# Second pass of a two-stage vision block: who issues the copies of the attention heads' operands

## The reference

```python
qkv = (x.reshape(B, L, dim) @ w_qkv + b_qkv).reshape(B, L, 3, nh, hd)
q = rot(q); k = rot(k)
attn = jnp.einsum('bnqd,bnkd->bnqk', q, k) * scale
rel_h = jnp.einsum('bnhwc,hkc->bnhwk', q6, bias_h)
rel_w = jnp.einsum('bnhwc,wkc->bnhwk', q6, bias_w)
attn = attn.reshape(B, nh, H, W, H, W) + rel_h[..., :, None] + rel_w[..., None, :]
attn = jax.nn.softmax(attn.reshape(B, nh, L, L), axis=-1)
out = jnp.einsum('bnqk,bnkd->bnqd', attn, v)
...
x = x + _L0_conv_ref(_gn(x), ...)
x = x + _L1_conv_ref(_gn(x), ...)
```

## Time and profile before

| | us |
|---|---|
| median of 3 runs | 3322.99 (3320.98 to 3324.75) |
| profiled execution, its own time | 3324.98 |
| its span, first to last instruction | 3323.2 |
| PE busy | 2701.7 (81%) |
| DVE busy | 2407.5 (72%) |
| ACT busy | 1554.1 (47%) |
| POOL busy | 1345.9 (41%) |
| mean granted TensorE clock | 0.932 |

### The profile page before, as it was taken

One profiled execution on the slowest core, in us unless ns is written; L12 is line 12 of the kernel. 1 busy time (PEld: TensorE's weight loads), 2 busy tenths in 40 slices (PEclk: granted clock), 3 DMA queues, 4 the chain that ended last, 5 costly groups with the idle time before them and its releaser, 6 DMA issues. The chain is left out here.

```text
span 3323.2 us, 40828 instructions
## 1 busy us (share of the span) xinstructions
PE 2701.7 (81%) x15888; PEld 1340.8 (40%) x15888; DVE 2407.5 (72%) x2270; ACT 1554.1 (47%) x1908; POOL 1345.9 (41%) x636
## 2 busy tenths in 40 slices
PE   3577777888778876777667998989888999989889
PEld 1222223333223332222223555546554555556555
DVE  1698899998999999999983555646554555636555
ACT  4445643556435564444431445525553445525554
POOL 4478766887668876766652100011000200011000
PEclk8799998998999999999896999999999999999999
DMA  2334444454444544445542112020021111020110
GB/s 68 120 120 133 146 144 142 133 138 154 148 144 128 139 158 143 161 133 145 178 136 68 22 33 52 10 62 11 23 52 40 32 33 28 25 71 1 33 52 20
DMA packets 96358, 297.46 MB, mean 90 GB/s; under 512 B 18860, under 2 KB 21432, under 8 KB 96152
## 3 DMA queue, kind: packets, MB, share of 16 engines
q1 hardware_dynamic: 96152, 294.68, 29.3%
HBM read 238.51 MB, written 23.07 MB: 79 GB/s over the span
## 5 line engine op out<-in xcount | busy, mean ns | idle before, releaser
L1605 POOL TENSOR_TENSOR arena<-arena 128x1024 f32<-128x1024 f32 x384 | 902.6, 2362 | 332.1 <-DVE arena L1093 280.6
L1093 DVE TENSOR_TENSOR_SCAN arena<-PS,arena 128x1024 f32<-128x1024 f32 x384 | 878.1, 2287 | 89.7 <-ACT PS L1442 63.8
L567 PE MATMUL PS<-arena,ident 128*128 128x512 f32 x1568 | 812.9, 645 | 20.5 <-ACT arena L1453 15.6
L1442 ACT ACTIVATE PS<-arena,a_inf,a_neg 128x1024 f32<-128x1024 f32 x384 | 463.8, 1208 | 777.0 <-DVE arena L1093 772.6
L1221 DVE CUSTOM_DVE_ANT_1 arena<-PS,arena 128x1024 f32<-128x1024 f32 x384 | 468.2, 1219 | 417.0 <-PE PS L852 415.4
L1530 ACT ACTIVATE arena<-arena,neg_max 128x1024 f32<-128x1024 f32 x384 | 440.9, 1148 | 577.9 <-DVE neg_max L1221 577.9
L558 PE MATMUL PS<-arena,sel 96*128 96x512 bf16 x768 | 247.0, 405 | 407.2 <-DVE arena L1101 403.8
L852 PE MATMUL PS<-arena 64*128 64x512 f32 x1536 | 448.5, 661 | 80.4 <-DMA arena<-arena 76.3
L1635 POOL TENSOR_TENSOR arena<-arena 128x512 f32<-128x512 f32 x48 | 68.4, 1424 | 1067.5 <-ACT arena L1499 1067.5
L1101 DVE TENSOR_TENSOR arena<-arena,PS 128x1024 f32<-128x1024 f32 x384 | 459.2, 1196 | 15.6 <-PE PS L558 13.9
L567 PEld LDWEIGHTS PS<-arena,ident 128*128 128x128 f32 x1568 | 319.6, 205 | 307.1 <-issue 250.2
(11 more groups left out here) (124 smaller groups left out, 2177.6 us busy)
## 6 DMA issues: line engine op xcount, KB each, us to landing
arena<-b_rows SPq DMA_DIRECT2D x256, 512.0 KB, 3.8
arena<-b_rows SPq DMA_DIRECT2D x256, 256.0 KB, 4.0
arena<-arena SPq DMA_DIRECT2D x216, 64.0 KB, 2.3
arena<-arena SPq DMA_DIRECT2D x96, 128.0 KB, 3.0
normed<-xn SPq DMA_DIRECT2D x5, 1536.0 KB, 6.4
normed<-x_in SPq DMA_DIRECT2D x4, 1536.0 KB, 7.6
residual<-x_in SPq DMA_DIRECT2D x4, 1536.0 KB, 8.3
x<-residual SPq DMA_DIRECT2D x4, 1536.0 KB, 6.4
```

Of the source, the lines that this page charges most:

```text
L567: last = pe.matmul(dst[:, half(h)], lhs, rhs[:, half(h)], start=start, stop=stop, skip_group_check=True)
L1093: dve.tensor_tensor_scan(HS[:, at % 2, ::step], DA[:, ::step], DBU[:, at % R3, ::step], 0.0, ALU.mult, ALU.add).then_inc(scan_done.sem, 1)
L1442: act.activation(DA, DELTA[:, tile % 2, :], ACT.Exp, bias=a_inf[:, col:col + 1], scale=a_neg[:, col:col + 1]).then_inc(da_ready.sem, 1)
L1605: pool.tensor_tensor(DBU[:, at % R3, :], DU[:, tile % 2, :], BSB[:, at % R3, :], ALU.mult).then_inc(dbu_ready.sem, 1)
```

## The change

Heads 0 and 1 stay with SP. The ten DMAs of heads 2 and 3 are issued by POOL, with the same waits ahead of them, in its own program order: the q copies after its addition `n` = 1, the k and bias copies after `n` = 3, group 1 after `n` = 9 and group 2 after `n` = 11. `head_loaded[2]` and `head_loaded[3]` are moved ahead of the semaphores that are cleared for each image; they are kept over the images, so whoever waits for them compares with `(b * 30 + n) * 16`, a value that is computed from the loop's register.

```diff
-    def __init__(self, sem, unit=1):
-        self.sem, self.unit = sem, unit
+    def __init__(self, sem, unit=1, kept=None):
+        self.sem, self.unit, self.kept = sem, unit, kept
     def after(self, b, n):
-        return n * self.unit
+        return n * self.unit if self.kept is None else (b * self.kept + n) * self.unit
...
+        head_loaded = [None] * (HG // 2) + [
+            Signal(ctx.enter_context(nc.semaphore(f"head{j}_loaded")), 16, HEAD_DMAS * GROUPS) for j in range(HG // 2, HG)]
...
-        head_loaded = [signal(f"head{j}_loaded", HEAD_DMAS * GROUPS, 16) for j in range(HG)]
+        head_loaded[0:HG // 2] = [signal(f"head{j}_loaded", HEAD_DMAS * GROUPS, 16) for j in range(HG // 2)]
...
+        OWN_HEADS = {"sp": range(HG // 2), "pool": range(HG // 2, HG)}
...
                 for k, (ready, count) in enumerate(((rope_ready, 2), (rope_ready, 4), (rel_saved, 2))):
                     sp.wait_ge(ready.sem, ready.after(b, count))
-                    for j in range(HG):
+                    for j in OWN_HEADS["sp"]:
                         for dst, src in operands(0, j)[k]:
                             sp.dma_start(dst, src).then_inc(head_loaded[j].sem, 16)
                 for g in range(1, GROUPS):
                     sp.wait_ge(rope_ready.sem, rope_ready.after(b, ROPE_FOR[g]))
                     sp.wait_ge(rel_saved.sem, rel_saved.after(b, REL_FOR[g]))
-                    for j in range(HG):
+                    for j in OWN_HEADS["sp"]:
...
+                def load_first(k):
+                    ready, count = ((rope_ready, 2), (rope_ready, 4), (rel_saved, 2))[k]
+                    pool.wait_ge(ready.sem, ready.after(b, count))
+                    for j in OWN_HEADS["pool"]:
+                        for dst, src in operands(0, j)[k]:
+                            pool.dma_start(dst, src).then_inc(head_loaded[j].sem, 16)
+                def load_group(g):
+                    pool.wait_ge(rope_ready.sem, rope_ready.after(b, ROPE_FOR[g]))
+                    pool.wait_ge(rel_saved.sem, rel_saved.after(b, REL_FOR[g]))
+                    for j in OWN_HEADS["pool"]:
+                        pool.wait_ge(s_psum.sem, s_psum.after(b, STEPS * g - HG + j + 1))
+                        for dst, src in itertools.chain(*operands(g, j)):
+                            pool.dma_start(dst, src).then_inc(head_loaded[j].sem, 16)
...
+                    if n in (1, 3):
+                        load_first(n // 2)
+                    if n == 3:
+                        load_first(2)
+                    if n in (9, 11):
+                        load_group(1 if n == 9 else 2)
```

More of the change, by code:

```diff
@@ L375, in build, with operands @@
         LATE_AT = {2 * m + 2: job for m, job in enumerate(LATE) if job}
+        def operands(g, j):
+            copies = [[], [], [(QX[2 * HD * h + HD:2 * HD * h + 2 * HD, j, :], RELC[j::HG, g // 2, :])
+                               for h in range(2)]]
+            for h in range(2):
+                for odd in range(2):
+                    at = XT * odd + HALF_HEAD * j
+                    rows = slice(2 * HD * h + HALF_HEAD * odd, 2 * HD * h + HALF_HEAD * (odd + 1))
+                    copies[0].append((QX[rows, j, :], QKC[at:at + HALF_HEAD, PLACE[g, "q"], :]))
+                    copies[1].append((KX[rows, j, :], QKC[at:at + HALF_HEAD, PLACE[g, "k"], half(h)]))
+            return copies
+        OWN_HEADS = {"sp": range(HG // 2), "pool": range(HG // 2, HG)}
         def norm_count(g, h):
```

## The result

The changed kernel takes 3296.6 us (median of 4 runs, 3295.6 to 3303.1) against 3323.4 before: a ratio of 0.9924, 95% interval 0.9907 to 0.9941. It is 27 us faster where 12 us slower was forecast.

A forecast was written before the change was run, and what follows sets the result against it. Bound: SP's issuing of 40 DMAs at each of eight group changes. Changes +14, image starts -3, register waits +1 make +12 us on the 3323 us median: 3335 us, range 3262 to 3412 (eight in ten).

The forecast's parts named there:

- What bounds the kernel: At eight group changes s35 waits for the end of SP's 40 issues; at most 63 us and some 10 of slow clock.
- The cost of one issue on POOL: T, time of one DMA issue on POOL: taken as 1.1 us, so eight changes cost +14 us; break-even 1.01 us.
- The form 3.4 + 20 T: Time in us from s30 to s35 at a group change, T being one POOL issue; 23.7 us before the change.
- the floor: Group changes with heads 2 and 3 in time, s33 as late as before: -63 and -10 us, at T 0.59.
- the DMA engines as the bound: Rival: both queues would not even double the engines' 0.44 share; later landing under 0.5 us a change, 4 us; no chance given.
- Heads 0 and 1 are issued when they were ... s33 stays as late as it is: SP at a group change loses its last 20 issues; head 0 in time, s33 unchanged; this part alone moves nothing.
- The start of an image: V's last copy holds s0; POOL's eight DMAs delay n=2 by 8 T; 0.8 us earlier each, four images -3 us.
- POOL is free at the changes: Between its addition and next multiplication POOL idles 86 us; what is queued behind its twenty DMAs isn't hurt.
- the waits on registers: Six PE waits per image compare with a computed value, 0.034 us a register move: 24 of them cost 1 us.
- the neighbouring case of T = 0.8: POOL issue at 0.8 us: a change takes 19.4 us, changes -34, starts -4, clock -2, total 3283 us.
- One wait of 8 to 10 us ahead of s35: Forecast's mark in the profile at group changes, in place of the waits of 3.2 and 3.6 us.
- the first rival: At the eight changes POOL issues below break-even, T below 0.99: faster, 3283 us at 0.8, 3246 at 0.59; chance 0.37.

The follow-up runs named there:

- e10: e6 with SP's 1.5 MB load of the next image's input put behind the completion of head 3 of group 2; 3215.2 us, ratio 0.9664.
- e3: Changed kernel, but at a change of group POOL waits until SP's head 1 is complete before issuing its DMAs; 3329.4 us.
- e4: Changed kernel, but POOL's copies at the changes of group move only the first quarter of the columns; 3273.4 us.
- e5: Changed kernel, but POOL issues the DMAs of all four heads and SP none; 3282.5 us.
- e1: Changed kernel, but heads dealt in turns: SP issues heads 0 and 2, POOL heads 1 and 3; 3247.5 us, ratio 0.9777.
- e6: Changed kernel, but at changes SP issues four and POOL six copies of every head, at starts POOL only the k copies; 3233.2 us, ratio 0.973.
- e7: Changed kernel, but SP issues all of group 0 at image starts, POOL only at the changes of group; 3283.0 us.
- e8: e1's heads in turns at the changes; at image starts POOL issues only the k copies, SP the q and bias copies; 3251.1 us.
- e11: Changed kernel with SP's 1.5 MB load of the next image put behind the completion of all heads of group 2; 3297.4 us.

## Why the prediction was wrong, point by point

*What bounds the kernel* was right: the end of SP's list in eight places. In e10 no `scores` waits for a DMA at a change; from s28 to s40 the eight take 262.9 us instead of 366.8, 104 of the 108 us between the two spans; the starts give 2.8.

*The cost of one issue on POOL* is the first step that failed. It was taken as 1.1 us, the middle between rows of another engine and 0.04 from what the two latencies of the Trainium skill ("DMA: Bandwidth & Descriptors", Specifications) give as a ratio; it is 0.487 us, with 0.491 from one to the next (9.83 us for 20). The value lay below the lower bound, 0.54, since SP's issue was no floor for another engine's. The page's figure is a time to the first byte, and no interval between issues can be had from it: the measurement decides. The sign of the forecast hung on this value, as the prediction says itself.

*The form 3.4 + 20 T* with T = 0.49 gives 13.2 us for s30 to s35, so the floor would hold: -63 - 10 us for the changes, -4 for the starts, 3246 us. The changed kernel got 27 of these 77 us. The second step that failed is the sentence on the DMA engines as the bound: "the share of 0.44 would not even double", and under 0.5 us a change. It was reckoned with T = 1.1. With 0.49 it more than doubles: a copy takes 0.44 x 0.67 = 0.29 us of all engines by the earlier trace rows, and 0.29/0.64 + 0.29/0.49 = 1.05, beside 1.10 and 1.04 in the windows. The sum says that the engines fill, but it fits better than it should: 64 KB each at both rates would be 236 GB/s, and the windows moved 162 and 135, in longer packets. A faster new queue thus harms the old one more. At a change it cost s33 18.4 to 21.6 us instead of 16.3 to 17.2, 3.2 on average, and at a start 2.8 us. e3, e4 and e5 each take the overlap or its bytes away, and each time the median landing falls to 2.3 to 2.7 us.

*"Heads 0 and 1 are issued when they were ... s33 stays as late as it is"* was wrong in its second half for that reason: issued at the same time, complete 3 us later. The Trainium skill says in the same page, section Issuing engines are not separate DMA queues, that the DMAs of all issuing engines run on the same 16 DMA engines and "interleave with each other"; the trace agrees (share 1.10, SP's copy 7.22 us to land behind POOL's). Of that section the prediction used the sentence on issue time and not this one.

*The start of an image*: V holds s0, as said. Eight POOL issues between n=1 and n=2 took 3.9 us instead of 8.8. The loss came from where none was seen, the bias copies of two queues, 1 MB together: -3 us were forecast for the four starts, and +11.2 were measured. The landing of the last copies was put at 2.3 us there, while the kernel before had already taken up to 4.2 us for its last bias copies.

*POOL is free at the changes; the waits on registers cost nothing visible*: right.

*The range* (3262 to 3412) held the measured time only by luck, through the neighbouring case of T = 0.8: T is not 0.8, and a cheaper issue and a later landing happen to add up to the same. "One wait of 8 to 10 us ahead of s35" is not there; "s34 and s35 without DMA waits: the first rival" is, and that rival's sign was right.

What stays open: the 6.7 us behind the last issue (the same 10.2 us from the end of that issue to the end of the span in e1, e3, e4, but 3.6 in e6, 4.1 in e7 and 3.5 before; it follows neither the number of POOL's DMAs nor their kind), the stops of 1.6 to 2.8 us in POOL's queue (one place each in e5, e6, e7, e8 and e10, none seen in the changed kernel), the slower packets of the changed kernel against e1, and the rest of the spread of 1 to 3 us between equal places when both queues are busy.

## What to carry to other kernels

What the second issuing queue took away here is issue time, and nothing else. Multiply the engines' share at the place by the new rate before you count a gain, and look at how far apart the copies land now. Where the share comes near 1, deal the copies so that both queues work on what is needed next, not each on its own half. When a list ends earlier, look at what its engine issues next: in e6 a 1.5 MB load moved up among copies that were still under way. And a price that no row shows is best bounded by what decides, not by the rows at hand: one kernel with a single such DMA would have given T, and with it the sign.

## What the runs showed of the hardware

- A DMA of 32 to 128 KB from SBUF to SBUF is issued at the changes of the changed kernel by GpSimd in 0.484 to 0.557 us, median 0.487, and by SyncE in a median of 0.592 us, 0.540 at the least, with single ones of up to 1.7 us.
- When one queue issues alone, its copies land in a median of 2.3 us (SyncE's, kernel before) and 2.4 us (GpSimd's, e5). With both queues issuing copies of 32 to 128 KB side by side the share of the engines was 1.04 to 1.10 at 135 to 162 GB/s in one change, and the median landing over all eight 3.7 (SyncE's) and 4.8 us (GpSimd's); the longest was 7.2 us on both, and 10.2 on GpSimd's where a load of 1.5 MB ran beside it (7.2 in e11 without).
- Eight copies of 128 KB, issued 0.64 us apart by SyncE alone, landed 0.83 us apart on average (starts of an image, kernel before).
- GpSimd's queue now and then stood still for 1.6 to 2.8 us between two DMAs or ahead of its first (e5, e6, e7, e8, e10); in e5, e7 and e8 the profile names nothing that it waited for.
- In the wait of 7.2 us ahead of s33 TensorE's granted clock fell from 1.00 to the 1.2 GHz level: 0.54 in the window 2325 to 2329, in which it did nothing, 0.50 in the next and 1.00 from 2337 on. The scores of s33 took 2.08 us instead of 1.13.
